# Row sums of the fifth turn: from VectorE's reduction to adds on GpSimd and one sum on TensorE, with VectorE squaring every fourth unit, in a two-layer graph kernel

## The chip, the cores and the metric

The kernel runs on one core of one Trainium2 chip. The metric is the device time of one execution in microseconds; for the kernel before it is 596.5 us, the median of three runs (594.94 to 597.69).

## The reference

Two layers over x (4096 x 128) with one dense matrix adj (4096 x 4096, float32). h is the row-normalized x, cut at zero; r is an element of adj.

```python
# layer 0
msg = h @ W + B
sens = exp(-(1.0 / r - 1.0) ** 2 / (2.0 * 0.5 * 0.5))
x = x + where(r < 1.0, sens, 0.0) @ msg
# layer 1, with h from the new x
A_hat = adj + eye(N)
d_inv_sqrt = sum(A_hat, axis=1) ** (-0.5)
x = x + relu((d_inv_sqrt[:, None] * A_hat * d_inv_sqrt[None, :]) @ (h @ W.T))
```

Layer 1 needs the row sums of adj, and it needs adj a second time, with rows of layer 1's h that exist only once layer 0 is done for those rows.

## The kernel before, in words

adj is cut into 64 units of 512 x 512 elements, held as 128 partitions x 2048. Eight turns of eight units each go through the matrix by blocks of 512 rows; turn g (counted from 0) takes the units u = 8g to 8g+7, in the column order of ORDER. The "fifth turn" is g = 4, units 32 to 39. `idx` is a unit's place in its turn. Two units are loaded as one pair into one of three buffers `raw` (SyncE's queue, 16 transfers a pair, `load`). The order of work on every engine is written out by hand in a loop over u; the engines meet only by semaphores.

For each unit:

- VectorE turns it (`turn`, line 665) from `raw` into one of four buffers `kept`, as soon as the buffer's earlier unit has been stored or used, and cuts it (`cut`, line 680): wt = v where v < 1, else 0, read as two inputs from `kept`.
- ScalarE makes the weight in place in `wt` (five buffers): logarithm (`log`, line 546), exp of its negative, which is 1/r (`invert`, line 551), the square of 1/r - 1 (`square`, line 556) and the last exp (`weigh`, line 565). For some units VectorE makes the square instead (`quad`, line 686, an operation of the shape of the cut, after `invert`), and `weigh` has another bias (line 562). `squared_by_dve` picks them: one in four of the first turn, one in two of the next three, none later.
- TensorE multiplies the weights with msg into the bank acc0, two units behind (`multiply_weights`, line 394), and in the same loop does layer 1's products (`mix_once`, line 407) for those units of `kept` whose columns are ready, or (`mix_late`, line 417) for units that were spilled to HBM and are loaded again.
- SyncE stores the units to be used again (`store`, line 307); GpSimd issues the late loads (line 362) in the order of LOADED, each after the buffer's earlier use is done (`late_done`).

The row sums are made in two ways. In the first four turns (PE_SUMS = 4) TensorE adds each unit of `kept` by a product with a matrix of ones (`sum_tiles`, line 425); ScalarE copies the bank (`copy_sums`, line 573), and TensorE turns the sums into rows (`turn_sums`, line 432). From the fifth turn on VectorE reduces each pair from `raw` (`row_sum`, line 673), and a small product (`sum_quads`, line 440) joins the parts. A `raw` buffer is free for the next load when both units are turned and, from the fifth turn on, also summed.

Between the turns stands a chain on the rows just finished: ScalarE copies acc0 (`copy_x1t`, line 591), TensorE transposes (`turn_x1`, line 448), VectorE adds to x and takes the moments (`make_x1`, lines 762 to 780), TensorE transposes again (`turn_hid`, line 454), ScalarE copies (`copy_hid`, line 603), TensorE multiplies with the second weight matrix (`multiply_support`, line 460) and VectorE scales (`make_support`, lines 690 to 791). `own_rows` (lines 748 to 756) takes the row sums up before `make_x1`. STEPS gives the place in the turn of each of these. After the last unit the remaining late units are multiplied and the eight row blocks are finished.

Of the kernel before, what the change touches and what calls it, by code (L numbers as in the profile page):

```python
# [5 lines left out]
P = 128  # L6
# [68 lines left out]


PE_SUMS = 4


def squared_by_dve(u):  # L80

    return u < PE_SUMS * G and u % (4 if u < G else 2) == (3 if u < G else 1)

# [34 lines left out]
def slot_before(j):  # L118

    return max((i for i in range(j) if late_slot(i) == late_slot(j)), default=None)  # L120


# [5 lines left out]
def build(nc, x, adj, w0, b0, w1, out):  # L128
# [6 lines left out]
    with ctx:  # L135
# [25 lines left out]
        late = sb("late", [P, LATE, T, ROWS])  # L161
        wt = sb("wt", [P, WTS, T, ROWS])
        x1t = sb("x1t", [D, ROWS])
        hid = sb("hid", [P, T, D])
# [32 lines left out]
        msg_bank = [mix[4], mix[5]]  # L197
        sum_bank = [mix[0], mix[3], mix[4], mix[5]]

# [30 lines left out]
        square_done = sem("square_done")  # L230
        quad_done = sem("quad_done")
        tiles_summed = sem("tiles_summed")
        sums_copied = sem("sums_copied")
# [53 lines left out]
        def _(sp):  # L287
            def load(n):
                g = n // C4
                if n >= RAW:  # L290
                    if n - RAW >= PE_SUMS * C4:
                        sp.wait_ge(summed, n - RAW + 1 - PE_SUMS * C4)
                    sp.wait_ge(turned, 2 * (n - RAW + 1))
                for e in range(0, 16, 4):
                    for q in (0, 2, 1, 3):
                        sp.dma_start(raw[q * B:(q + 1) * B, n % RAW, e:e + 4],  # L296
                                     adj_parts[g // 2, g % 2, col(2 * n) // 2, q, :, e:e + 4]
                                     ).then_inc(raw_loaded[n % RAW], 16)
# [36 lines left out]
        def _(pool):  # L335
# [14 lines left out]

            for j, (r, c) in enumerate(LOADED):
                slot = late_slot(j)
                u = r * G + ORDER[r].index(c)
                before = slot_before(j)
                if before is not None:
                    pool.wait_ge(late_done, before + 1)
                elif slot >= LATE:
                    last_pair = max(n for n in range(PAIRS) if n % RAW == (slot - LATE) // 2)
                    pool.wait_ge(summed, last_pair + 1 - PE_SUMS * C4)
                    pool.wait_ge(turned, 2 * last_pair + 2)  # L360
                pool.wait_ge(spilled[u % KEPT], 16 * spill_count(u))
                pool.dma_start(late_tile(slot).rearrange("p k i -> p (k i)"),  # L362
                               spill[r, c]).then_inc(late_loaded[slot], 16)

        @block.tensor
        def _(pe):
# [54 lines left out]
            def sum_tiles(u):  # L421
# [5 lines left out]
                mm.then_inc(tiles_summed, 1)  # L427

            def turn_sums(g):
                pe.wait_ge(sums_copied, g + 1)  # L430
# [5 lines left out]
            def sum_quads(g):  # L436
                pe.wait_ge(summed, C4 * (g + 1 - PE_SUMS))
                if g == PE_SUMS:
                    pe.wait_ge(quads_done, 2)
# [31 lines left out]
            for u in range(UNITS):  # L471
                g, idx = u // G, u % G
                if g == 0 and idx % 2 == 0:
                    turn_h0(idx // 2)
                    multiply_msg(idx // 2)
                if g > PE_SUMS and step_at(g, idx, "sum_quads"):
                    sum_quads(g - 1)
# [6 lines left out]
                if g >= 1 and idx < LAG:  # L484
                    multiply_weights(u - LAG)
                if 1 <= g <= PE_SUMS and step_at(g, idx, "sum_quads"):
                    turn_sums(g - 1)
# [54 lines left out]
        def _(act):  # L542
# [24 lines left out]
            def copy_sums(g):  # L567
                act.wait_ge(tiles_summed, G * (g + 1))
                if g == 0:
# [45 lines left out]
            for u in range(UNITS):  # L615
# [9 lines left out]
                if g == 0 and idx in (1, 3, 5):  # L625
                    std_rows((idx + 1) // 2)
                    copy_h0((idx + 1) // 2)
                if 1 <= g <= PE_SUMS and idx == 0:
                    copy_sums(g - 1)
# [22 lines left out]
        def _(dve):  # L652
            def turn(u):
# [3 lines left out]
                if u >= KEPT:  # L657
# [3 lines left out]
                    if at_once(v):  # L661
                        dve.wait_ge(once_done, once_count(v))
                dst = kept[:, u % KEPT].rearrange("p k (e i) -> p e k i", i=B)
                src = raw[:, n % RAW].rearrange("p e (k h i) -> p e k h i", k=T, h=2)[:, :, :, h, :]
                nc.vector.transpose(dst, src).then_inc(turned, 1)  # L665

            def row_sum(n):
                g, jp = n // C4, n % C4
                if g >= PE_SUMS + 2 and jp == 0:
                    dve.wait_ge(quads_summed, g - 1)  # L670
# [72 lines left out]
            def own_rows(g):  # L743
                dve.wait_ge(quads_summed, g + 1)
                if g >= 1:
                    dve.wait_ge(newton, 3 * g)
                if g < PE_SUMS:
                    nc.vector.tensor_copy(pows[:, 0, :], side[:, 0:T]).then_inc(rows_owned, 1)
                    dve.wait_ge(rows_owned, g + 1)
                    return  # L750
                if g == PE_SUMS:
                    dve.wait_ge(quads_done, 2)
# [6 lines left out]
            def make_x1(g):  # L759
# [16 lines left out]
                last.then_inc(hid_done, 1)  # L776
                if g >= PE_SUMS:
                    dve.wait_ge(rows_summed, g + 1 - PE_SUMS)
                nc.vector.tensor_scalar(pows[:, 0, :], pows[:, 0, :], 1.0, None, ALU.add)
# [17 lines left out]
            for u in range(UNITS):  # L797
                g, idx = u // G, u % G
                turn(u)
                if g < PE_SUMS or u < PE_SUMS * G + 2:  # L800
                    cut(u)
                    if u >= 1 and squared_by_dve(u - 1):
                        quad(u - 1)
                if idx % 2 == 1 and g >= PE_SUMS:
                    row_sum(u // 2)
# [4 lines left out]
                elif g == 0:  # L810
                    make_msg(idx // 2)
                if u >= PE_SUMS * G + 2:
                    cut(u)
# [62 lines left out]
```

## Time and profile before

| | |
|---|---|
| median of three runs | 596.5 us (594.94 to 597.69) |
| the profiled execution: its time, its span | 593.92 us, 592.1 us |
| TensorE matmul busy | 528.7 us (89%) |
| VectorE busy | 472.2 us (80%) |
| ScalarE busy | 462.4 us (78%) |
| GpSimd busy | 41.4 us (7%) |
| row sums on VectorE (line 673), 16 | 70.1 us |
| cuts on VectorE (line 680), 64 | 146.5 us |
| squares on ScalarE (line 556), 50; on VectorE (line 686), 14 | 94.9 us; 32.0 us |
| sums on TensorE (line 425), 256 records | 35.1 us |

Of the profiled execution the profile shows the busy time of each engine, the chain of work that ended last, the groups of instructions by line, and timelines. Times are from the span's start. DVE is VectorE, ACT ScalarE, PE TensorE, POOL GpSimd. A float32 matmul appears as two records, so "x8" is one unit's four products. Busy time is an average over stages with different limits.

### The profile page before, as it was taken

How to read it: one execution, taken by the hardware profiler on the slowest of the kernel's cores; microseconds unless marked ns; L12 is line 12 of the kernel's file. 1: busy time of each engine (PE TensorE's matmuls, PEld its weight loads, DVE VectorE, ACT ScalarE, POOL GpSimd, SP SyncE). 2: the span in 40 equal slices, each digit the busy share in tenths (PEclk: the TensorE clock that was granted, in tenths of full speed). 3: DMA queues.
4: the chain of work that ended last, by engine and by line, in shares of the span. 5: the costliest groups of instructions: out<-in, count | busy, mean ns of one | idle time of the engine just before them, and what ended most of it. 6: DMA issues, size and time to landing. Idle time of an engine off the chain costs nothing.

```text
span 592.1 us, 4974 instructions
## 1 busy us (share of the span) xinstructions
PE 528.7 (89%) x1579; PEld 239.3 (40%) x1579; DVE 472.2 (80%) x552; ACT 462.4 (78%) x305; POOL 41.4 (7%) x68
## 2 busy tenths in 40 slices
PE   2458796979989999999979998989999999999994
PEld 1244433323433444344434444434444444445452
DVE  5899988999899898999999599995999379003156
ACT  2299899999999999998999949999699948900010
POOL 0343300000000000000000000000000000201000
PEclk9759897999999999999979999999999999999998
DMA  6999999999999999979989959994888220399122
GB/s 170 223 234 318 331 330 336 344 326 295 367 323 339 346 344 260 303 232 355 231 192 315 254 163 251 343 261 104 213 213 214 71 71 6 137 424 361 66 71 71
DMA packets 93340, 145.19 MB, mean 245 GB/s; under 512 B 10369, under 2 KB 84354, under 8 KB 84354
## 3 DMA queue, kind: packets, MB, share of 16 engines
q1 hardware_dynamic: 88274, 108.17, 66.8%
q0 software_dynamic: 5040, 36.70, 16.6%
q8 instruction: 12, 0.20, 0.1%
q14 instruction: 14, 0.11, 0.1%
HBM read 106.04 MB, written 38.80 MB: 245 GB/s over the span
## 4 chain that ended last, share of the span: by engine, by line
PE 45%; ACT 23%; DVE 15%; SPq 8%; issue 5%; DMA 3%; DVEq 0%
PE acc L394 17%; PE mix L417 12%; PE mix L407 10%; SPq L296 7%; ACT wt L546 6%; ACT wt L551 6%; DVE kept L665 6%; ACT wt L556 5%; ACT wt L565 5%; DVE wt L680 3%; DVE rowpart L673 2%; DMA adj_t_spill<-kept 2%; PE acc L417 2%; PE mix L425 1%; DVE wt L686 1%
## 5 line engine op out<-in xcount | busy, mean ns | idle before, releaser
L394 PE MATMUL acc<-wt,msg 128*128 128x512 f32 x512 | 238.1, 609 | 15.8 <-ACT wt L565 8.9
L394 PEld LDWEIGHTS acc<-wt,msg 128*128 128x128 f32 x512 | 95.7, 193 | 146.1 <-issue 121.3
L665 DVE STREAM_TRANSPOSE kept<-raw 128x2048 f32<-128x2048 f32 x64 | 147.4, 2304 | 6.9 <-DMA adj_t_spill<-kept 5.1
L680 DVE SCALAR_TENSOR_TENSOR wt<-kept 128x2048 f32<-128x2048 f32 x64 | 146.5, 2288 | 1.7
L546 ACT ACTIVATE wt<-wt 128x2048 f32<-128x2048 f32 x64 | 121.7, 1902 | 19.9 <-DVE wt L680 19.9
L551 ACT ACTIVATE wt<-wt 128x2048 f32<-128x2048 f32 x64 | 121.6, 1900 | 0.5
L407 PE MATMUL mix<-kept,support 128*128 128x512 f32 x224 | 101.2, 595 | 1.7 <-DVE kept L665 1.7
L565 ACT ACTIVATE wt<-wt 128x2048 f32<-128x2048 f32 x50 | 95.0, 1899 | 0.0
L556 ACT ACTIVATE wt<-wt 128x2048 f32<-128x2048 f32 x50 | 94.9, 1897 | 0.0
L417 PE MATMUL mix<-late,support 128*128 128x512 f32 x208 | 93.5, 593 | 1.3 <-DVE support L791 1.3
L673 DVE TENSOR_REDUCE rowpart<-raw 128x16 f32<-128x4096 f32 x16 | 70.1, 4380 | 0.0
L407 PEld LDWEIGHTS mix<-kept,support 128*128 128x128 f32 x224 | 41.8, 190 | 54.4 <-issue 51.6
L417 PEld LDWEIGHTS mix<-late,support 128*128 128x128 f32 x208 | 39.2, 190 | 49.9 <-issue 49.9
L362 POOL DMA_DIRECT2D late<-adj_t_spill x26 | 13.9, 535 | 454.6 <-PE mix L417 375.4
L425 PE MATMUL mix<-kept,ones 128*32 128x512 f32 x256 | 35.1, 621 | 9.4 <-DVE kept L665 9.4
L762 DVE TENSOR_TENSOR x<-side,x 128x512 f32<-128x512 f32 x8 | 5.5, 686 | 43.2 <-PE side L448 43.2
L686 DVE SCALAR_TENSOR_TENSOR wt<-wt 128x2048 f32<-128x2048 f32 x14 | 32.0, 2287 | 7.0 <-ACT wt L551 6.9
L603 ACT COPY hid_t<-side 128x512 f32<-128x512 f32 x8 | 4.6, 574 | 29.5 <-PE side L454 29.5
L649 ACT COPY kept<-mix 128x512 f32<-128x512 f32 x6 | 3.5, 585 | 29.9 <-PE mix L417 26.6
L562 ACT ACTIVATE wt<-wt 128x2048 f32<-128x2048 f32 x14 | 26.5, 1895 | 0.0
L347 POOL TENSOR_SCALAR support<-x,mv 128x128 f32<-128x128 f32 x24 | 21.9, 928 | 40.1 <-DVE mv L705 40.1
L830 DVE TENSOR_TENSOR kept<-mix,support 128x512 f32<-128x512 f32 x6 | 4.1, 689 | 19.2 <-PE mix L508 19.2
(87 smaller groups left out, 254.2 us busy)
## 6 DMA issues: line engine op xcount, KB each, us to landing
raw<-in_adj_dram SPq DMA_DIRECT2D x512, 128.0 KB, 6.3
adj_t_spill<-kept SPq DMA_DIRECT2D x35, 1024.0 KB, 9.8
late<-adj_t_spill POOLq DMA_DIRECT2D x26, 1024.0 KB, 8.4
raw<-adj_t_spill POOLq DMA_DIRECT2D x9, 1024.0 KB, 9.1
x<-in_x_dram SPq DMA_DIRECT2D x32, 64.0 KB, 2.7
out_dram<-kept SPq DMA_DIRECT2D x32, 64.0 KB, 1.8
w_sb<-in_L_gnn_W_dram SPq DMA_DIRECT2D x1, 64.0 KB
late<-in_L_gnn_W_dram SPq DMA_DIRECT2D x1, 64.0 KB
```

The source lines that it names most:

```text
L296: sp.dma_start(raw[q * B:(q + 1) * B, n % RAW, e:e + 4], adj_parts[g // 2, g % 2, col(2 * n) // 2, q, :, e:e + 4]).then_inc(raw_loaded[n % ...
L394: mm = nc.tensor.matmul(acc0[:], msg[:, col(u) * T + k, :], wt[:, u % WTS, k, :], start=(first and k == 0), stop=(last and k == T - 1))
L407: mm = nc.tensor.matmul(once_bank[g][:], support[:, c * T + k, :], kept[:, u % KEPT, k, :], start=(first and k == 0), stop=False)
L417: mm = nc.tensor.matmul(bank[:], support[:, c * T + k, :], late_tile(slot)[:, k, :], start=(start and k == 0), stop=(stop and k == T - 1))
L425: mm = nc.tensor.matmul(bank[k * B:(k + 1) * B, :], ones[:], kept[:, u % KEPT, k, :], start=(u % G == 0), stop=(u % G == G - 1))
L546: nc.scalar.activation(v, v, ACT.Ln, bias=LN_GUARD).then_inc(ln_done, 1)
L551: nc.scalar.activation(v, v, ACT.Exp, scale=-1.0).then_inc(inv_done, 1)
L556: nc.scalar.activation(v, v, ACT.Square, bias=-1.0).then_inc(square_done, 1)
L565: nc.scalar.activation(v, v, ACT.Exp, scale=-2.0).then_inc(wt_done, 1)
L665: nc.vector.transpose(dst, src).then_inc(turned, 1)
L673: nc.vector.tensor_reduce(dst, src, AX_X, ALU.add).then_inc(summed, 1)
L680: nc.vector.scalar_tensor_tensor(out=wt[:, u % WTS], in0=v, scalar=CUTOFF, in1=v, op0=ALU.is_lt, op1=ALU.mult).then_inc(cut_done, 1)
```

## The change

PE_SUMS stays 4 and a second bound DVE_SUMS = 5 takes its place wherever it says from which turn on VectorE reduces the rows. In the fifth turn GpSimd adds the turned units of `kept` up in a new buffer `row_acc` (128 x 2048, float32): seven adds, the first of units 32 and 33. Each waits for its unit to be turned and for the add before. TensorE then sums `row_acc` by one product with ones into the bank mix[5] (`sum_total`) at unit 40, after the weights' product; ScalarE copies it and TensorE turns it, as in the earlier turns. VectorE's `turn` of unit u, when unit u - 4 is one that GpSimd adds, waits for that add. VectorE makes the square of the units 35 and 39. The late loads of GpSimd's queue are issued from the same loop over the units, each placed by `load_unit` at the unit after that whose product frees its buffer, before that unit's add. SyncE's loads that follow the fifth turn's pairs no longer wait for a row sum. The dynamic DMA scratch is set to 8192 bytes, half of what it was, which makes room for `row_acc`.

```diff
 PE_SUMS = 4
+DVE_SUMS = PE_SUMS + 1
+
+def added_by_pool(u):
+    return PE_SUMS <= u // G < DVE_SUMS
+
+def adds(u):
+    return max(1, u % G)
 
 def squared_by_dve(u):
-    return u < PE_SUMS * G and u % (4 if u < G else 2) == (3 if u < G else 1)
+    return u < DVE_SUMS * G and u % (4 if u < G or added_by_pool(u) else 2) == (3 if u < G or added_by_pool(u) else 1)
...
+def load_unit(j):
+    before = slot_before(j)
+    if before is None:
+        return G + 2 + j
+    return [u for u in sorted(JOBS) for _ in JOBS[u]][before] + 1
...
+        row_acc = sb("row_acc", [P, T, ROWS])
...
-        sum_bank = [mix[0], mix[3], mix[4], mix[5]]
+        sum_bank = [mix[0], mix[3], mix[4], mix[5], mix[5]]
...
-                    if n - RAW >= PE_SUMS * C4:
-                        sp.wait_ge(summed, n - RAW + 1 - PE_SUMS * C4)
+                    if n - RAW >= DVE_SUMS * C4:
+                        sp.wait_ge(summed, n - RAW + 1 - DVE_SUMS * C4)
                     sp.wait_ge(turned, 2 * (n - RAW + 1))
...
-            for j, (r, c) in enumerate(LOADED):
+            def add(u):
+                pool.wait_ge(turned, u + 1)
+                if adds(u) >= 2:
+                    pool.wait_ge(pool_added, adds(u) - 1)
+                first = kept[:, (u - 1) % KEPT] if u % G == 1 else row_acc[:]
+                nc.gpsimd.tensor_tensor(row_acc[:].rearrange("p k i -> p (k i)"),
+                                        first.rearrange("p k i -> p (k i)"),
+                                        kept[:, u % KEPT].rearrange("p k i -> p (k i)"),
+                                        ALU.add).then_inc(pool_added, 1)
+
+            def load_late(j):
+                r, c = LOADED[j]
...
+            for u in range(G, UNITS):
+                for j in range(len(IN_TURN)):
+                    if load_unit(j) == u:
+                        load_late(j)
+                if added_by_pool(u) and u % G >= 1:
+                    add(u)
+            for j in range(len(IN_TURN), len(LOADED)):
+                load_late(j)
...
+            def sum_total():
+                pe.wait_ge(pool_added, G - 1)
+                for k in range(T):
+                    mm = nc.tensor.matmul(sum_bank[PE_SUMS][k * B:(k + 1) * B, :], ones[:], row_acc[:, k, :],
+                                          start=True, stop=True)
+                mm.then_inc(tiles_summed, 1)
...
+                if u == DVE_SUMS * G:
+                    sum_total()
-                if 1 <= g <= PE_SUMS and step_at(g, idx, "sum_quads"):
+                if 1 <= g <= DVE_SUMS and step_at(g, idx, "sum_quads"):
                     turn_sums(g - 1)
...
-                act.wait_ge(tiles_summed, G * (g + 1))
+                act.wait_ge(tiles_summed, G * (g + 1) if g < PE_SUMS else G * PE_SUMS + 1)
...
-                if 1 <= g <= PE_SUMS and idx == 0:
+                if 1 <= g <= DVE_SUMS and idx == 0:
                     copy_sums(g - 1)
...
                     if at_once(v):
                         dve.wait_ge(once_done, once_count(v))
+                    if added_by_pool(v):
+                        dve.wait_ge(pool_added, adds(v))
...
-                if g < PE_SUMS or u < PE_SUMS * G + 2:
+                if g < DVE_SUMS or u < DVE_SUMS * G + 2:
                     cut(u)
                     if u >= 1 and squared_by_dve(u - 1):
                         quad(u - 1)
-                if idx % 2 == 1 and g >= PE_SUMS:
+                if idx % 2 == 1 and g >= DVE_SUMS:
                     row_sum(u // 2)
...
-    nc = _bacc.Bacc("TRN2", target_bir_lowering=False, num_devices=1)
+    nc = _bacc.Bacc("TRN2", target_bir_lowering=False, num_devices=1, dynamic_dma_scratch_size=8192)
```

In `sum_quads`, `row_sum`, `own_rows`, `make_x1` and the late loads' waits PE_SUMS becomes DVE_SUMS in the same way.

## Rows read from the trace of the kernel before

**Rows 1.** The chain of waits, 296 to 360 us: start us, us, what.

```profile
300.37 2.29 DVE wt L680
302.69 1.91 ACT wt L546
304.60 1.80 ACT wt L556
...
329.80 0.47 ACT x1t L591
330.27 0.14 issue
330.41 3.67 PE acc L394 x8
```

**Rows 2.** Stretches: busy time of each engine, granted TensorE clock, DMA.

```profile
core 0: us, PE busy (x) PEld busy (x) DVE busy (x) ACT busy (x) POOL busy (x), PEclk, DMA share, GB/s
249.00:302.00 53.00, 48.09 (x129) 22.07 (x127) 52.59 (x43) 50.04 (x32) 1.58 (x3) 0.99 0.93 260
398.00:490.00 92.00, 91.22 (x229) 41.73 (x230) 72.72 (x66) 76.40 (x49) 2.64 (x5) 1.00 0.57 147
...
302.00:308.50 6.50, 6.42 (x8) 2.75 (x9) 6.46 (x4) 5.84 (x5) 0.00 (x0) 0.52 0.98 237
```

**Rows 3.** VectorE: its groups in 253 to 303 us, then its timeline.

```profile
L673 DVE TENSOR_REDUCE rowpart<-raw 128x16 f32<-128x4096 f32 x4 | 17.6, 4388 | 0.0
L665 DVE STREAM_TRANSPOSE kept<-raw 128x2048 f32<-128x2048 f32 x7 | 16.1, 2304 | 0.0
...
251.16 2.29 DVE L680 SCALAR_TENSOR_TENSOR wt<-kept 128x2048 f32<-128x2048 f32 x1
...
271.16 0.68 DVE L762 TENSOR_TENSOR x<-side,x 128x512 f32<-128x512 f32 x1
...
274.13 2.30 DVE L665 STREAM_TRANSPOSE kept<-raw 128x2048 f32<-128x2048 f32 x1
...
287.40 0.16 DVE L690 TENSOR_TENSOR tmp<-inv 128x8 f32<-128x8 f32 x1
...
289.30 2.30 DVE L665 STREAM_TRANSPOSE kept<-raw 128x2048 f32<-128x2048 f32 x1
```

**Rows 4.** ScalarE: a group of 249 to 303 us, and its timeline.

```profile
L546 ACT ACTIVATE wt<-wt 128x2048 f32<-128x2048 f32 x8 | 15.2, 1904 | 3.6 <-DVE wt L680 3.6
...
253.83 0.57 ACT L573 COPY hid_t<-mix 128x512 f32<-128x512 f32 x1
```

**Rows 5.** TensorE's timeline, 228 to 308 us.

```profile
228.44 1.06 PE L425 MATMUL mix<-kept,ones 128*32 128x512 f32 x8
...
259.39 0.95 PE L432 MATMUL side<-thirty_second,hid_t 128*128 128x1 f32 x8
...
276.49 3.70 PE L407 MATMUL mix<-kept,support 128*128 128x512 f32 x8 [1.43 <-DVE kept L665]
...
302.08 6.76 PE L394 MATMUL acc<-wt,msg 128*128 128x512 f32 x8 [3.29 <-ACT wt L565]
```

**Rows 6.** GpSimd's timeline, the first 2 us.

```profile
0.24 0.10 POOL L865 MEMSET const-float32-0.0<- 128x1 f32 x1 [0.24 <-issue]
...
0.74 0.20 POOL L336 MEMSET ident<- 128x128 f32 x1 [0.29 <-POOLq L865]
...
1.22 0.28 POOL L341 TENSOR_SCALAR_AFFINE_SELECT ident<-ident 128x128 f32<-128x128 f32 x1
```

**Rows 7.** GpSimd's line 347 (ns min/median/max); 28 to 29 us of it; VectorE beside it.

```profile
L347 POOL TENSOR_SCALAR support<-x,mv x24: 702/710/2474, 24.7 to 62.8; 128x128 f32<-128x128 f32 x24
...
L347 POOL TENSOR_SCALAR support<-x,mv 128x128 f32<-128x128 f32 x1 | 2.5, 2452 | 0.0
...
27.06 2.29 DVE L680 SCALAR_TENSOR_TENSOR wt<-kept 128x2048 f32<-128x2048 f32 x1
```

**Rows 8.** GpSimd's timeline, late loads of the fifth turn.

```profile
256.42 0.53 POOL L362 DMA_DIRECT2D late<-adj_t_spill  x1 [41.10 <-PE mix L417]
264.18 0.53 POOL L362 DMA_DIRECT2D late<-adj_t_spill  x1 [7.23 <-PE mix L417]
271.49 0.53 POOL L362 DMA_DIRECT2D late<-adj_t_spill  x1 [6.78 <-PE mix L417]
```

More of the change, by code:

```diff
@@ L231, in build @@
         quad_done = sem("quad_done")
+        pool_added = sem("pool_added")
         tiles_summed = sem("tiles_summed")
@@ L358, in _ @@
                     last_pair = max(n for n in range(PAIRS) if n % RAW == (slot - LATE) // 2)
-                    pool.wait_ge(summed, last_pair + 1 - PE_SUMS * C4)
+                    pool.wait_ge(summed, last_pair + 1 - DVE_SUMS * C4)
                     pool.wait_ge(turned, 2 * last_pair + 2)
@@ L436, in sum_quads @@
             def sum_quads(g):
-                pe.wait_ge(summed, C4 * (g + 1 - PE_SUMS))
-                if g == PE_SUMS:
+                pe.wait_ge(summed, C4 * (g + 1 - DVE_SUMS))
+                if g == DVE_SUMS:
                     pe.wait_ge(quads_done, 2)
@@ L475, in _ @@
                     multiply_msg(idx // 2)
-                if g > PE_SUMS and step_at(g, idx, "sum_quads"):
+                if g > DVE_SUMS and step_at(g, idx, "sum_quads"):
                     sum_quads(g - 1)
@@ L668, in row_sum @@
                 g, jp = n // C4, n % C4
-                if g >= PE_SUMS + 2 and jp == 0:
+                if g >= DVE_SUMS + 2 and jp == 0:
                     dve.wait_ge(quads_summed, g - 1)
@@ L746, in own_rows @@
                     dve.wait_ge(newton, 3 * g)
-                if g < PE_SUMS:
+                if g < DVE_SUMS:
                     nc.vector.tensor_copy(pows[:, 0, :], side[:, 0:T]).then_inc(rows_owned, 1)
@@ L750, in own_rows @@
                     return
-                if g == PE_SUMS:
+                if g == DVE_SUMS:
                     dve.wait_ge(quads_done, 2)
@@ L776, in make_x1 @@
                 last.then_inc(hid_done, 1)
-                if g >= PE_SUMS:
-                    dve.wait_ge(rows_summed, g + 1 - PE_SUMS)
+                if g >= DVE_SUMS:
+                    dve.wait_ge(rows_summed, g + 1 - DVE_SUMS)
                 nc.vector.tensor_scalar(pows[:, 0, :], pows[:, 0, :], 1.0, None, ALU.add)
@@ L811, in _ @@
                     make_msg(idx // 2)
-                if u >= PE_SUMS * G + 2:
+                if u >= DVE_SUMS * G + 2:
                     cut(u)
```

## The prediction

> **What bounds the kernel now.** I read the chain of waits first, then the stretches, then the timelines of single engines around the fifth turn (units 32 to 39). Up to the cut of unit 39 the chain lies on VectorE; it then passes to ScalarE, whose work is back to back until the copy of x1's transpose, and at 330.4 us to TensorE [rows 1]. From there TensorE is the limit for most of what is left (in 398 to 490 us it is busy 91.2 of 92 us [rows 2]), so a shift of the point 330.4 moves the end by about as much. In 249 to 302 us VectorE is busy 52.6 of 53 us, TensorE 48.1, ScalarE 50.0 [rows 2]. There VectorE makes four row sums of 4.4 us, 17.6 in all, and its transposes wait for nothing, so neither loads nor spills are late [rows 3]. ScalarE loses 3.6 us to late cuts in that turn [rows 4]. TensorE stands idle 3.3 us before unit 37's product, which then takes 6.76 us where unit 36's at 276.49 took 3.70 [rows 5]: the granted clock is 0.52 there, the lower of its two levels [rows 2]. That is 3.1 us more, though TensorE catches up: at 330.4 it waits 0.75 us for ScalarE (the chain's copy ends at 330.3).
>
> **The change, part by part.** *VectorE*: minus four row sums, 17.6 us; plus two squares of the cut's shape, 2 x 2.3 = 4.6. Net 13.0 us less, if nothing holds it. *ScalarE*: minus two squares of 1.8 us (the steps of the chain [rows 1]); plus one copy of the sums, 0.5 [rows 4]; and the 3.6 us of waits go if cuts are on time: at most 3.6 + 3.6 - 0.5 = 6.7 us before the copy of x1's transpose in unit 42's place. *TensorE*: plus one sum of the total, 1.06, and the turning of the sums, 0.95; minus a small product of the partial sums, taken as nothing: +2.0 us [rows 5]. Against that stand the 3.3 us idle, the 3.1 of low clock and the 1.4 us it waited for unit 36's transpose [rows 5], 7.8 in all: TensorE could be 5.8 us early, plus the 0.75 it waits: 6.5. *Halved scratch*: descriptor space of GpSimd's DMAs; no row shows it full or waited for. I take nothing; a loss would fall on the burst of loads at the end.
>
> *GpSimd*: seven adds of 128x2048. The trace has none. Its memset of one element takes 0.10 us and of 128 elements 0.20, so 0.8 ns for an element written; the select of 128, one read and one write, 0.28, so 1.4 ns [rows 6], and 0.6 for the read. Two reads and a write: 2.0 ns x 2048 = 4.2 us. Ends: 2.3 us, if it ran as fast as VectorE's cut [rows 7], and 11.2, sixteen times the 0.70 us that its tensor_scalar of 128 elements takes [rows 7], nearly all of it a fixed part. I take 4.2, from the rows nearest in kind. At 7.2 us a unit (four chain steps of ScalarE) GpSimd keeps up.
> The Trainium skill (GPSIMD Engine Reference, section 3) gives 4.5 us for exactly this add; by it the sum below would be 1.5 us longer. No row here shows it.
>
> *Order on GpSimd's queue*: the adds of units 33, 34 and 35 stand behind the late loads 6, 7 and 8, which wait for TensorE and go out at 256.4, 264.2 and 271.5 [rows 8]. So these adds begin from 257.0, 264.7 and 272.0. VectorE's new waits (unit 36 may not overwrite its buffer before unit 32 is added, and so on) lie 7 us and more behind these, and cost nothing while an add is under 7 us. TensorE's sum of the total waits for the last add and stands behind unit 38's product, about 314 us; the last add ends by 307. The next late load (job 9) has its turn after that.
>
> *Sharing between GpSimd and VectorE*, the term that decides. Eight tensor_scalars of GpSimd run beside VectorE; in each batch one takes 2.47 us instead of 0.70, and it is the one in flight during the cut, which takes its usual 2.29 [rows 7]. So a cut (two inputs in SBUF) shuts GpSimd out until it ends. Whether GpSimd, once reading, shuts the cut out, no row shows: the instruction in flight as the cut began can have finished its 128 reads. Lower bound: no delay to VectorE. Upper bound: a whole add for each add that meets a cut or a square. Since the port is visibly held for a whole instruction and not shared element by element, I take it to be held both ways.
> The Trainium skill (SBUF — State Buffer, "Who interferes with whom") says that whoever issues first has the shared pair for its whole instruction and that two SBUF inputs contend with GpSimd's reads. Rows 7 agree for the one direction. It speaks against this change.
>
> **The sum with the port held both ways, add 4.2 us.** Start at the cut of unit 33, 251.2 [rows 3]; without row sums, transpose and cut are 4.55 us a unit. Unit 34's cut ends at 258.0; add 33 holds the port to 262.2. Unit 35's cut waits for the previous turn's sums (TensorE from 259.4, a little under 0.95 us [rows 5]) and ends at 265.0; add 34 to 269.2, beside make_x1, 3.0 us (271.16 to 274.13 [rows 3]), and transpose 36. Cut 36 ends 272.5, add 35 holds to 276.7, then square 35 (whose input ScalarE has ready by about 275) to 279.0, add 36 to 283.2, cut 37 to 285.5, add 37 to 289.7. The small two-input steps of make_support meet that and its 1.9 us (287.40 to 289.30 [rows 3]) begin only then: 291.6. Cut 38 ends 296.1, add 38 at 300.3, cut 39 at 302.6: 302.66 now [rows 1]. So the four row sums taken away are given back whole. On: add 39 to 306.8, cut 40 to 309.0, square 39 to 311.3, cut 41 to 315.8, the row sum of the sixth turn's first pair to 320.1, cut 42 to 324.6. ScalarE takes up unit 42 at 324.65; now it does 5.4 us (three steps) before 329.8, at 324.4. Shift +0.3. TensorE would idle again before units 38's and 37's products and pay low clock once more, but reaches 330.4 just in time. Sum: 593.9 (the profiled execution) + 0.4 = 594.3; that execution is 2.6 below the median of the three runs, so against the median 596.5 + 0.4, about **596.9**. Five adds in a row lie on this path (35 to 39), so it moves by 5 us for each microsecond of the add: 4.5 gives +1.8, 3.7 gives -2.2.
>
> **Rivals.** *VectorE is never held by GpSimd* (adds fit in the gaps). Then cut 39 is done by about 293, well before ScalarE wants it, and square 39 waits for ScalarE's inverse at 302.7: cut 41 ends at 309.5, and after row sum and transpose cut 42 at 318.4, while ScalarE, 6.7 us early, would take it at 324.4 - 6.7 = 317.7. The loss of 0.7 leaves 6.0 us, and TensorE's 6.5 lets that stand: 596.5 - 6.0 = **590.5**. For: all three cuts that began beside a GpSimd instruction took 2.29. Against: the shut-out in the other direction is complete.
> *A long add, both ways held* (the slower side). Mechanism: the chain add, cut, add of units 35 to 39. It decides from where (A - 4.2) x 5 passes 3 us, an add of 4.8. At 5.5 us: +6.5 + 0.4, **603.4**; an idle TensorE at low clock could add its 3.1. For: GpSimd's spans here have big fixed parts (0.70 for 128 elements). Against: GpSimd's memset and select scale gently.
> *GpSimd too late altogether*: an add of over 7.2 us would stall VectorE's transposes at unit 38 on; each microsecond above costs at least five. Toward the upper end of 11.2 that is over 620. I give this 2 in 100.
>
> **How the numbers follow.** About 0.5% (3 us) is what a measurement of this kernel can tell from no change. Held both ways with an add of 3.7 to 4.8: 0.50, own range 594 to 600, of it 0.06 faster, 0.36 same, 0.08 slower. Never held: 0.36, own range 588.5 to 593.5, of it 0.33 faster, 0.03 same. Long add: 0.12, slower; too late 0.02, slower. Together faster 0.39, same 0.39, slower 0.22. Same and faster weigh alike; I forecast the single likeliest case, 596.9. The range must reach the never-held case, and leaves out its lowest part and the long adds above 5.2 us: 589 to 602.
>
> **What would show it.** In the changed profile: cuts and squares of the fifth turn longer than 2.29 us or beginning over 2 us after the transpose; GpSimd adds of 4.2 us and, where they meet a cut, 6.5; spacing of transposes near 7 us in spite of the missing row sums; the cut of unit 39 ending near 302 against 293 in the never-held case. The step at 330.4 shifts by under 3 us or by -6. ScalarE's waits for cuts stay near 3.6 us or vanish. I am wrong in the mechanism if cuts keep 2.29 with no gap while adds run, and wrong in a term if adds alone take over 5 or under 3.5. If the time falls or rises with the first 330 us unchanged, it lies in the tail, and the scratch or the order of the late loads would be suspect.

## The result, and the profile after

The changed kernel takes 602.04 us (median of four, 598.1 to 604.31) where the kernel before, run beside it, takes 596.3. The ratio is 1.0098, 95% interval 1.0068 to 1.0128: slower by 5.8 us. The forecast was 596.9, range 589 to 602; the time lies above it.

The profiled execution of the changed kernel is the fastest of its four (598.1 us); its span is 596.3 us, that of the kernel before 592.1. Its fifth turn begins earlier: unit 32's transpose starts at 239.64, in the trace before at 240.96. Single executions differ by more than that up to there (unit 34's transpose starts at 252.06 here, and at 254.32 in a kernel below that has the same program so far). So 1.3 us are added to the times after when the two are compared.

VectorE's groups of the changed kernel in 249 to 303 us (columns as in [rows 3]):

```profile
L733 DVE SCALAR_TENSOR_TENSOR wt<-kept 128x2048 f32<-128x2048 f32 x7 | 21.9, 3123 | 0.2
L718 DVE STREAM_TRANSPOSE kept<-raw 128x2048 f32<-128x2048 f32 x7 | 16.1, 2302 | 0.0
L739 DVE SCALAR_TENSOR_TENSOR wt<-wt 128x2048 f32<-128x2048 f32 x1 | 6.6, 6624 | 0.0
L743 DVE TENSOR_TENSOR tmp<-inv 128x8 f32<-128x8 f32 x1 | 4.5, 4516 | 0.0
L827 DVE TENSOR_SCALAR hid<-x,mv 128x128 f32<-128x128 f32 x4 | 3.1, 838 | 0.0
```

The row sums are gone. In their place a cut (line 733) takes 3.12 us on average, the square of unit 35 (line 739) 6.62 and a step on 8 elements (line 743) 4.52. VectorE's timeline, with unit 36 first:

```profile
265.85 3.12 DVE L827 TENSOR_SCALAR hid<-x,mv 128x128 f32<-128x128 f32 x4
...
269.04 2.29 DVE L718 STREAM_TRANSPOSE kept<-raw 128x2048 f32<-128x2048 f32 x1
271.37 6.09 DVE L733 SCALAR_TENSOR_TENSOR wt<-kept 128x2048 f32<-128x2048 f32 x1
277.38 6.62 DVE L739 SCALAR_TENSOR_TENSOR wt<-wt 128x2048 f32<-128x2048 f32 x1
283.93 2.30 DVE L718 STREAM_TRANSPOSE kept<-raw 128x2048 f32<-128x2048 f32 x1
286.26 2.29 DVE L733 SCALAR_TENSOR_TENSOR wt<-kept 128x2048 f32<-128x2048 f32 x1
288.47 4.52 DVE L743 TENSOR_TENSOR tmp<-inv 128x8 f32<-128x8 f32 x1
...
297.07 2.29 DVE L733 SCALAR_TENSOR_TENSOR wt<-kept 128x2048 f32<-128x2048 f32 x1
...
301.62 4.31 DVE L733 SCALAR_TENSOR_TENSOR wt<-kept 128x2048 f32<-128x2048 f32 x1
```

And GpSimd's timeline beside it: add 34, the late load ahead of add 35, then adds 35, 36 and 37 one by one:

```profile
263.45 4.85 POOL L378 TENSOR_TENSOR row_acc<-row_acc,kept 128x2048 f32<-128x2048 f32 x1
270.17 0.57 POOL L395 DMA_DIRECT2D late<-adj_t_spill  x1 [1.87 <-PE mix L459]
270.76 4.54 POOL L378 TENSOR_TENSOR row_acc<-row_acc,kept 128x2048 f32<-128x2048 f32 x1
275.44 6.41 POOL L378 TENSOR_TENSOR row_acc<-row_acc,kept 128x2048 f32<-128x2048 f32 x1
286.31 6.65 POOL L378 TENSOR_TENSOR row_acc<-row_acc,kept 128x2048 f32<-128x2048 f32 x1 [4.46 <-DVE kept L718]
```

Lay the two side by side. Add 35 starts at 270.76, 0.6 us ahead of cut 36; the cut ends when the add's 4.5 us and its own 2.2 have gone by. Add 36's record starts at 275.44; it waits for the cut to end at 277.5 and then runs to 281.85; only then does square 35 run, which ends at 284.0, 6.6 us after it started. Where VectorE comes first it is GpSimd that waits: add 37 starts with cut 37 and takes 6.65 us. Line 378's shortest add, never held, is the 4.54 us of unit 35. Not every operation is held: beside add 34 the addition to x (0.68 us) and the statistics (0.87 for four) take what they took before, and transposes keep 2.30 us beside the adds.

The sum up to the end of cut 38, against the trace before: three row sums less (3 x 4.3 = 12.9), one square more (2.3), a new wait of 2.4 us for the previous turn's sums at unit 34, and held time of 3.8 (cut 36), 4.3 (square 35), 2.3 (hid) and 4.4 us (line 743), 14.8 in all: 14.8 + 2.4 + 2.3 - 12.9 = 6.6. Measured: 299.36 + 1.3 against 293.93 is +6.7. TensorE follows:

```profile
286.28 5.40 PE L449 MATMUL mix<-kept,support 128*128 128x512 f32 x8 [4.78 <-DVE kept L718]
291.52 3.60 PE L436 MATMUL acc<-wt,msg 128*128 128x512 f32 x8
297.09 3.70 PE L449 MATMUL mix<-kept,support 128*128 128x512 f32 x8 [1.98 <-DVE kept L718]
...
306.76 5.40 PE L436 MATMUL acc<-wt,msg 128*128 128x512 f32 x8 [2.53 <-ACT wt L616]
...
318.95 1.06 PE L474 MATMUL mix<-row_acc,ones 128*32 128x512 f32 x8
...
334.68 3.60 PE L436 MATMUL acc<-wt,msg 128*128 128x512 f32 x8
```

The last product starts unit 40's weights; it answers to 330.41 in [rows 1] and comes 4.3 + 1.3 = 5.6 us later. Most of that is ScalarE's lateness, which comes from the cuts: its copy of x1's transpose starts at 333.55, in the trace before at 329.71, which is 5.1 us later. The last 0.5 us is TensorE's: from 306.76 on it has no gap, with the sum of the total and the turning of the sums added (1.8 us), while the product at 306.76 is 1.8 us slow (5.40 against 3.60) where it was 3.1 before. The granted clock of the 6 us with that product is 0.72 on average, so a part of them lies at the lower of the two levels (columns as in [rows 2]):

```profile
306.00:312.00 6.00, 5.24 (x9) 2.23 (x10) 5.96 (x2) 6.00 (x4) 4.33 (x1) 0.72 1.07 247
```

From there to the end nothing is added: the span is 4.2 us longer, plus 1.3 is 5.5, close to the 5.8 of the ratio.

### The profile page after: what moved, and what is told of

The parts are those of the page before. It is cut to its first block, busy times and chain, and to the rows that moved or that the text cites. A ratio compares the mean times of both kernels' runs of the same rounds, so it can differ in the third digit from the quotient of the medians.

```text
span 596.3 us, 5012 instructions
## 1 busy us (share of the span) xinstructions
PE 532.4 (89%) x1593; PEld 239.1 (40%) x1593; DVE 478.4 (80%) x549; ACT 459.9 (77%) x304; POOL 82.5 (14%) x75
## 4 chain that ended last, share of the span: by engine, by line
PE 54%; ACT 18%; DVE 13%; SPq 6%; DMA 4%; issue 2%; POOL 2%; DVEq 0%; POOLq 0%
PE acc L436 21%; PE mix L459 14%; PE mix L449 12%; SPq L318 5%; ACT wt L597 5%; ACT wt L602 5%; DVE kept L718 4%; ACT wt L616 4%; ACT wt L607 4%; DVE wt L733 3%; DMA adj_t_spill<-kept 3%; DVE wt L739 2%; PE mix L467 2%; POOL row_acc L378 2%; PE acc L459 2%
## 5 line engine op out<-in xcount | busy, mean ns | idle before, releaser
L733 DVE SCALAR_TENSOR_TENSOR wt<-kept 128x2048 f32<-128x2048 f32 x64 | 154.3, 2412 | 1.8
L449 PE MATMUL mix<-kept,support 128*128 128x512 f32 x224 | 102.9, 603 | 6.8 <-DVE kept L718 6.8
L726 DVE TENSOR_REDUCE rowpart<-raw 128x16 f32<-128x4096 f32 x12 | 52.6, 4381 | 0.0
L739 DVE SCALAR_TENSOR_TENSOR wt<-wt 128x2048 f32<-128x2048 f32 x16 | 40.9, 2558 | 7.1 <-ACT wt L602 7.0
L467 PE MATMUL mix<-kept,ones 128*32 128x512 f32 x256 | 36.7, 647 | 7.4 <-DVE kept L718 7.4
L378 POOL TENSOR_TENSOR row_acc<-row_acc,kept 128x2048 f32<-128x2048 f32 x6 | 35.5, 5920 | 8.9 <-DVE kept L718 8.6
```

Of the source, the lines that this page charges most:

```text
L449: mm = nc.tensor.matmul(once_bank[g][:], support[:, c * T + k, :], kept[:, u % KEPT, k, :], start=(first and k == 0), stop=False)
L467: mm = nc.tensor.matmul(bank[k * B:(k + 1) * B, :], ones[:], kept[:, u % KEPT, k, :], start=(u % G == 0), stop=(u % G == G - 1))
L726: nc.vector.tensor_reduce(dst, src, AX_X, ALU.add).then_inc(summed, 1)
L733: nc.vector.scalar_tensor_tensor(out=wt[:, u % WTS], in0=v, scalar=CUTOFF, in1=v, op0=ALU.is_lt, op1=ALU.mult).then_inc(cut_done, 1)
L739: nc.vector.scalar_tensor_tensor(out=v, in0=v, scalar=-2.0, in1=v, op0=ALU.add, op1=ALU.mult).then_inc(quad_done, 1)
```

## Experiments

The theory: GpSimd and VectorE share a way into SBUF (the port, below) that one instruction holds; a GpSimd instruction that reads holds up those of VectorE's that need it. The rivals put the loss on what else changed: the order on GpSimd's queue, the new waits, the halved scratch, TensorE's added work, the squares. Each ratio below is to the kernel before on the same chip, with its 95% interval.

**Adds of 128 elements.** (On the changed kernel, as all that follow unless the text says otherwise.) The other 1920 elements of each unit's sums are left out.

```diff
-                nc.gpsimd.tensor_tensor(row_acc[:].rearrange("p k i -> p (k i)"),
-                                        first.rearrange("p k i -> p (k i)"),
-                                        kept[:, u % KEPT].rearrange("p k i -> p (k i)"),
-                                        ALU.add).then_inc(pool_added, 1)
+                nc.gpsimd.tensor_tensor(row_acc[:, 0, 0:128], first[:, 0, 0:128],
+                                        kept[:, u % KEPT, 0, 0:128], ALU.add).then_inc(pool_added, 1)
```

> The changed kernel, but each of GpSimd's seven adds covers only 128 of the 2048 elements (the rest of the fifth turn's row sums is left out; the total is filled with ones at the start). Everything else of the change stays: the order of the late loads on GpSimd's queue, the new waits, TensorE's sum of the total, the halved scratch, VectorE's two squares. Theory (an add of GpSimd that has begun holds VectorE's two-input operations until it ends): nothing long is held, cuts and squares of the fifth turn are back at 2.29 us, and the time falls below the kernel before, to about 590.5 us (ratio to before 0.99). Rival (the loss comes from what stays): about 602 us, ratio 1.01.

Measured: 589.83 us, ratio 0.9909 (0.9876 to 0.9941). Line 734 is the cut, min/median/max in ns over all 64; then the groups of the square, of hid and of the small step in 245 to 302 us:

```profile
L734 DVE SCALAR_TENSOR_TENSOR wt<-kept x64: 2276/2292/2294, 20.1 to 495.5; 128x2048 f32<-128x2048 f32 x64
```

```profile
L740 DVE SCALAR_TENSOR_TENSOR wt<-wt 128x2048 f32<-128x2048 f32 x2 | 4.6, 2293 | 3.0 <-ACT wt L603 3.0
...
L828 DVE TENSOR_SCALAR hid<-x,mv 128x128 f32<-128x128 f32 x4 | 0.9, 283 | 0.0
...
L744 DVE TENSOR_TENSOR tmp<-inv 128x8 f32<-128x8 f32 x1 | 0.4, 422 | 0.0
```

No cut is held. Everything else of the change together is a gain of 0.9%, and the length of the adds costs about 11 us (1.0098 against 0.9909). This is the prediction's never-held case, 590.5. It throws out the rivals of scratch, TensorE's work and the order of issue. Small adds also end VectorE's new waits sooner and let the late loads through sooner; that these are not the cause is read from the trace with the full adds: VectorE has no idle time before any transpose of the fifth turn, and GpSimd, its adds done, still waits for TensorE before each late load (1.87 us before the one at 270.17, 13.6 before the first one after the adds).

**The scratch alone**, on the kernel before.

```diff
-    nc = _bacc.Bacc("TRN2", target_bir_lowering=False, num_devices=1)
+    nc = _bacc.Bacc("TRN2", target_bir_lowering=False, num_devices=1, dynamic_dma_scratch_size=8192)
```

> The kernel before with nothing changed but the dynamic DMA scratch halved to 8192 bytes. Theory: no change, ratio 1.000 within 0.3%, and the nine or so late loads issued at the end keep their 0.53 us spacing. Rival (smaller descriptor space delays GpSimd's loads): slower by 2 us or more, with longer load instructions in the last 90 us.

Measured: 595.12 us, ratio 0.9988 (0.9972 to 1.0003). The nine loads into `raw` at the end take 530 ns each, before 528. No cost can be told.

**Adds of 1024 elements.** Half of the fifth turn's sums is left out.

```diff
-                nc.gpsimd.tensor_tensor(row_acc[:].rearrange("p k i -> p (k i)"),
-                                        first.rearrange("p k i -> p (k i)"),
-                                        kept[:, u % KEPT].rearrange("p k i -> p (k i)"),
-                                        ALU.add).then_inc(pool_added, 1)
+                nc.gpsimd.tensor_tensor(row_acc[:, 0:2].rearrange("p k i -> p (k i)"),
+                                        first[:, 0:2].rearrange("p k i -> p (k i)"),
+                                        kept[:, u % KEPT, 0:2].rearrange("p k i -> p (k i)"),
+                                        ALU.add).then_inc(pool_added, 1)
```

> As the changed kernel, but each add covers 1024 of 2048 elements (half of the fifth turn's row sums is left out). An add then takes about 2.3 us, and fits beside a transpose of 2.3 us. Theory (port held both ways): most cuts are not held or by under 1 us, time 591 to 594 us. A loss that grows in proportion to GpSimd's busy time would give halfway between 590.5 and 602, 596 us. Rival (the loss comes from what stays): 602 us.

Measured: 590.94 us, ratio 0.9931 (0.9908 to 0.9953). VectorE, the square of unit 35 and the small step:

```profile
280.06 2.46 DVE L742 SCALAR_TENSOR_TENSOR wt<-wt 128x2048 f32<-128x2048 f32 x1 [1.92 <-ACT wt L605]
...
286.99 2.33 DVE L746 TENSOR_TENSOR tmp<-inv 128x8 f32<-128x8 f32 x1
```

The holds are still there but short, 0.2 and 2.2 us, and VectorE has idle time to take them in (1.9 us before the square). The loss is not proportional to GpSimd's work: half the work costs some 1 us, which is within the two intervals, all of it about 11.

**A fill instead of an add, and a copy instead of an add.** Both leave the fifth turn's row sums out; the copy has one run.

The line that stands in the add's place, in the one kernel and in the other:

```diff
+                nc.gpsimd.memset(row_acc[:], 1.0).then_inc(pool_added, 1)
```

```diff
+                nc.gpsimd.tensor_copy(row_acc[:].rearrange("p k i -> p (k i)"),
+                                      kept[:, u % KEPT].rearrange("p k i -> p (k i)")).then_inc(pool_added, 1)
```

> As the changed kernel, but in place of each add GpSimd fills the 128x2048 buffer with a constant (the fifth turn's row sums are left out): a long GpSimd instruction that writes SBUF and reads nothing. If what is held is the reading side of the port, cuts and squares keep 2.29 us and the time is that of the tiny adds, about 590.5 us. If any long GpSimd instruction holds VectorE (writing side too), cuts stretch by what is left of the fill (estimated at 1.6 us from the 0.8 ns an element of the small fills) and the time lies at 592 to 595 us; if the loss is of the waits and the order, 602 us.

> As the changed kernel with a plain copy of each unit by GpSimd in place of the add (the fifth turn's row sums are left out): one input instead of two. If one read stream is enough to hold VectorE, the first small step of make_support, which takes 0.16 us in the kernel before, 0.16 with the fills and 4.52 with the full adds, takes 1 to 3 us, about as long as the copy; if only two inputs hold it, 0.16. Time 590 to 593 us in both cases.

Measured: the fill 590.39 us, ratio 0.9901 (0.9872 to 0.993); the copy 589.27. The seven fills (min/median/max in ns), unit 36's fill, and VectorE's square of unit 35, which starts while that fill runs:

```profile
L377 POOL MEMSET row_acc<- x7: 1806/1809/1828, 260.2 to 294.2; 128x2048 f32 x7
...
277.24 1.81 POOL L377 MEMSET row_acc<- 128x2048 f32 x1
```

```profile
278.01 2.29 DVE L735 SCALAR_TENSOR_TENSOR wt<-wt 128x2048 f32<-128x2048 f32 x1 [2.00 <-ACT wt L598]
```

The seven copies, and VectorE's timeline with the square of unit 35 and the small step:

```profile
L377 POOL COPY row_acc<-kept x7: 1896/2811/4017, 256.7 to 293.4; 128x2048 f32<-128x2048 f32 x7
```

```profile
274.50 3.93 DVE L736 SCALAR_TENSOR_TENSOR wt<-wt 128x2048 f32<-128x2048 f32 x1 [1.99 <-ACT wt L599]
...
282.90 1.85 DVE L740 TENSOR_TENSOR tmp<-inv 128x8 f32<-128x8 f32 x1
```

A fill of 1.81 us, which only writes, holds no cut or square and is held by none: the square above keeps 2.29 us, and the longest fill is 0.02 us longer than the shortest although some start beside cuts. (The small step, 0.16 us here, says nothing: the fill before it, 282.58 to 284.39, was over when it started at 284.77.) A copy, one read stream, both holds (the small step 1.85 us, the square 3.93) and is held (up to 4.02 us, against 1.90). So what is shared is on the reading side, and one stream on GpSimd's side is enough. The times do not tell the two apart, as expected; the durations do.

**The squares back on ScalarE**, the rest as changed.

```diff
-    return u < DVE_SUMS * G and u % (4 if u < G or added_by_pool(u) else 2) == (3 if u < G or added_by_pool(u) else 1)
+    return u < PE_SUMS * G and u % (4 if u < G else 2) == (3 if u < G else 1)
```

> The changed kernel without one part: ScalarE squares units 35 and 39 again, VectorE does not. Theory (an add holds two-input operations): in the changed kernel the square of unit 35 alone is held to 6.62 us and the cut behind it waits as well; without it the cut of unit 38 ends about 4.5 us earlier although ScalarE has 3.6 us more to do, most of it while it waited anyway: about 598 us, ratio to before 1.00. Rival (squares on VectorE are the useful part of the change, the adds the loss): 604 to 606 us.

Measured: 597.8 us, ratio 1.0039 (1.0022 to 1.0057). Cut 36 and cut 37:

```profile
273.64 6.11 DVE L733 SCALAR_TENSOR_TENSOR wt<-kept 128x2048 f32<-128x2048 f32 x1
279.68 2.30 DVE L718 STREAM_TRANSPOSE kept<-raw 128x2048 f32<-128x2048 f32 x1
282.01 4.32 DVE L733 SCALAR_TENSOR_TENSOR wt<-kept 128x2048 f32<-128x2048 f32 x1
```

Taking the squares away gives back some 3.5 of the 5.8 us (1.0098 to 1.0039), a little less than the theory's 4.5; cut 37 is now held by add 36 instead, for 2.0 us, since the transpose covers the rest. Here moving the squares to VectorE is a loss while full adds run beside them.

**Adds in two and in four pieces.** All sums computed. The edit for two pieces stands here; for four, 2 becomes 1.

```diff
+                for i in range(0, T, 2):
+                    last = nc.gpsimd.tensor_tensor(row_acc[:, i:i + 2].rearrange("p k i -> p (k i)"),
+                                                   first[:, i:i + 2].rearrange("p k i -> p (k i)"),
+                                                   kept[:, u % KEPT, i:i + 2].rearrange("p k i -> p (k i)"),
+                                                   ALU.add)
+                last.then_inc(pool_added, 1)
```

> The changed kernel, all of its sums computed, but each add is issued as two instructions of 1024 elements, about 2.3 us each. Theory (the port is held for one instruction and passed on when it ends): a cut waits for at most 2.3 us, VectorE has some 2 us to spare per unit where ScalarE sets the pace, so little of it shows: 592 to 596 us, ratio to before 0.993 to 1.0. Rival (GpSimd keeps the port as long as it has adds queued, or the loss follows GpSimd's total busy time, which stays): 602 us.

> As the last, with four instructions of 512 elements, about 1.2 us each and 0.1 to 0.3 us more for issuing them. Theory: a VectorE operation waits for at most 1.2 us; 591 to 594 us, ratio 0.99 to 0.995, at or below the two-part adds. If each instruction's fixed part (0.7 us for 128 elements) counts in full, GpSimd's adds take about 7 us a unit, VectorE's transposes come to wait for them: 600 us or more. Rival as before: 602 us.

Measured: 599.68 us, ratio 1.0067 (1.0044 to 1.009), and 600.1 us, ratio 1.0077 (1.0056 to 1.0098). Here the theory's detail failed: a cut was to wait for one piece at most. GpSimd's two pieces of unit 35's add, one by one, and VectorE's cut 36 and square 35, in two pieces:

```profile
274.30 2.38 POOL L379 TENSOR_TENSOR row_acc<-row_acc,kept 128x1024 f32<-128x1024 f32 x1
...
276.62 2.38 POOL L379 TENSOR_TENSOR row_acc<-row_acc,kept 128x1024 f32<-128x1024 f32 x1
```

```profile
274.85 6.31 DVE L735 SCALAR_TENSOR_TENSOR wt<-kept 128x2048 f32<-128x2048 f32 x1
281.09 4.45 DVE L741 SCALAR_TENSOR_TENSOR wt<-wt 128x2048 f32<-128x2048 f32 x1
```

The cut waits through both pieces, 4.0 us, although the first ends at 276.7. With four pieces the same cut takes 6.48 us. But the square behind it waits for one piece only (4.45 us in two pieces, 3.36 in four). So in these two traces pieces that follow one another without having been held keep VectorE out like one long add, while after GpSimd has itself been held the two take turns. Why it is so these runs do not show. In four pieces a plain copy of VectorE, 4 elements from SBUF to SBUF, is held too (0.17 us alone):

```profile
291.34 1.20 DVE L841 COPY dinv<-inv 128x4 f32<-128x4 f32 x1
```

Splitting gained 1 to 2 us of the 5.8, not the 6 to 11 that were expected, and the intervals overlap with that of the whole adds.

**Adds ahead of the late loads** on GpSimd's queue.

```diff
             for u in range(G, UNITS):
+                if added_by_pool(u) and u % G >= 1:
+                    add(u)
                 for j in range(len(IN_TURN)):
                     if load_unit(j) == u:
                         load_late(j)
-                if added_by_pool(u) and u % G >= 1:
-                    add(u)
```

> The changed kernel with each add ahead of the late load of the same unit on GpSimd's queue, so that the adds of units 33 to 35 are released by their transposes and not by TensorE. Theory (what is held depends on who comes first): add 35 then begins after cut 35 and no longer stands in front of cut 36 and the moments' steps; the cut of 36 (6.09 us in the changed kernel) shortens to 2.3 to 4.5 us, the cut of unit 38 ends 2 to 4 us earlier: 598 to 600 us. Rival (the port's total load decides, whatever the order): 602 us. Late loads 6 to 8 go out up to 5 us later; if TensorE comes to wait for them, above 602 us.

Measured: 599.66 us, ratio 1.0069 (1.0042 to 1.0096). VectorE:

```profile
257.14 4.32 DVE L733 SCALAR_TENSOR_TENSOR wt<-kept 128x2048 f32<-128x2048 f32 x1
...
264.34 3.69 DVE L733 SCALAR_TENSOR_TENSOR wt<-kept 128x2048 f32<-128x2048 f32 x1
...
275.52 2.29 DVE L733 SCALAR_TENSOR_TENSOR wt<-kept 128x2048 f32<-128x2048 f32 x1
277.73 6.63 DVE L739 SCALAR_TENSOR_TENSOR wt<-wt 128x2048 f32<-128x2048 f32 x1
```

Cut 36 falls from 6.09 to 2.29 us, and the cuts of units 34 and 35 are held instead, 2.0 and 1.4 us; the first falls into time that VectorE stood idle before (2.4 us, now 0.3). hid and square 35 are held as before (3.13 and 6.63 us). The order on the queue decides what is held. In the trace the cut of unit 38 ends 2.4 us sooner after unit 34's transpose; the two ratios' intervals overlap, so the time alone does not show it.

**The fifth turn's sums on TensorE alone** (a change of the kernel before: GpSimd out of it, VectorE squaring 35 and 39; units 32 and 33 are summed at unit 33, behind `turn_sums`, since ScalarE still reads the bank before; a transpose waits for the sum of the buffer's earlier unit).

```diff
-PE_SUMS = 4
+PE_SUMS = 5
...
+                if u == 33:
+                    sum_tiles(32)
+                    sum_tiles(33)
```

> The kernel before with the fifth turn's row sums on TensorE alone, as in the first four turns (units 32 and 33 summed at unit 33), VectorE squaring units 35 and 39 as in the change, GpSimd out of it. VectorE and ScalarE gain what the never-held case gave them (6.0 us), TensorE pays 8 sums of 1.0 us instead of its idle 3.3 and low clock 3.1 and waits of 1.4. Theory (without GpSimd's port nothing is held; TensorE becomes the bound of that turn): cuts 2.29 us, about 596 us or 1 less, ratio 0.995 to 1.0. If TensorE had more room than its idle time shows: 590.5 us. If TensorE's extra work costs in full on top of its old waits: 601 us.

Measured: 594.92 us, ratio 0.9987 (0.9963 to 1.001). The stretch of 249 to 302 us (columns as in [rows 2]):

```profile
249.00:302.00 53.00, 53.00 (x180) 22.51 (x179) 42.03 (x43) 48.87 (x32) 1.59 (x3) 1.00 1.01 279
```

TensorE is busy all of it, with a granted clock of 1.00 (its level of 2.4 GHz), and VectorE falls to 42.0 of 53 us, its cuts all at 2.29. The bound has gone to TensorE, and the gain is spent there: no change from the kernel before can be told.

**Shared by elements**: GpSimd adds 1024 elements of each unit, TensorE sums the other 1024. All sums computed.

```diff
+            def sum_half(u):
+                for k in (2, 3):
+                    mm = nc.tensor.matmul(sum_bank[PE_SUMS][k * B:(k + 1) * B, :], ones[:], kept[:, u % KEPT, k, :],
+                                          start=(u % G == 0), stop=(u % G == G - 1))
```

> All sums computed: GpSimd adds only the first 1024 elements of each unit of the fifth turn (2.3 us an add), TensorE sums the other 1024 (half a unit's sum, 0.5 us, eight times) and the total. Theory: holds are as rare as with the half adds alone (590.9 us), and TensorE pays 3.5 us more, of which about 0.7 shows, as in the all-TensorE version (7 us more work, 4.9 us longer than the tiny adds): 592.5 to 593.5 us, ratio to before 0.995. Rival (TensorE's and GpSimd's costs add up in full): 595 us, no better than all on TensorE.

Measured: 597.04 us, ratio 1.0026 (1.0008 to 1.0044), above the theory's 593 and the rival's 595. What stands out is on TensorE, two of the halves:

```profile
278.69 1.05 PE L475 MATMUL mix<-kept,ones 128*32 128x512 f32 x4
...
283.74 1.05 PE L475 MATMUL mix<-kept,ones 128*32 128x512 f32 x4
```

Two products into two groups of 32 rows take 1.05 us, as long as four into four groups (1.06 in [rows 5]). Half the sum saves TensorE nothing: it is busy 53.0 of the 53 us again, as in the version before, and the sum of the total and the short adds' holds (2.4 us on the square of 35) come on top. That these make up the 2 us over the version before was not tested.

**Shared by units**: TensorE sums units 32 to 35, GpSimd adds 36 to 39. All sums computed.

```diff
 def adds(u):
-    return max(1, u % G)
+    return max(1, u % G - G // 2)
...
-                if added_by_pool(u) and u % G >= 1:
+                if added_by_pool(u) and u % G >= G // 2 + 1:
                     add(u)
```

A product like `sum_tiles` sums units 32 to 35 into the bank, which stays open for the total.

> All sums computed: TensorE sums units 32 to 35 of the fifth turn (four sums of 1.0 us), GpSimd adds up units 36 to 39 (three adds of 4.5 us) and TensorE sums their total into the same bank. Theory: the holds at the moments' steps, the cut of unit 36 and the square of unit 35 are gone; what is left is one add on the first small step of make_support (4.5 us) and the two on the cuts of 39 and 40. TensorE has 4 us more to do than in the changed kernel and no idle before unit 36's product. The cut of unit 38 ends some 6 us earlier than in the changed kernel: 594 to 597 us, ratio to before 0.995 to 1.002. Rival (each add costs the same wherever it lies: 12 us over seven adds): 590.5 + 3 x 1.7 + 3 = 598.5 us.

Measured: 593.88 us, ratio 0.9956 (0.9932 to 0.9979). Cut 36, square 35 and the small step:

```profile
274.50 2.29 DVE L752 SCALAR_TENSOR_TENSOR wt<-kept 128x2048 f32<-128x2048 f32 x1
276.71 2.29 DVE L758 SCALAR_TENSOR_TENSOR wt<-wt 128x2048 f32<-128x2048 f32 x1
...
283.46 4.51 DVE L762 TENSOR_TENSOR tmp<-inv 128x8 f32<-128x8 f32 x1
```

The holds of unit 36 are gone; those at the small step and on the cuts of 39 and 40 (4.32 us each) are left. This beats both kernels, the one before by 0.4%, the changed one by 1.4%; a gain of 2.6 us, against the 5.4 of the tiny adds (0.9909), which are held up by nothing long.

## Why the prediction was wrong

It forecast no change, 596.9 us, and the time rose by 5.8 us. The mechanism it took was right; the order in which it laid the operations at the port was not.

- *The mechanism* was right: the port is held both ways. Its signs are there: stretched cuts and squares, and adds of 6.65 us where a cut came first. The case without holds was given 590.5 us; tiny adds give 589.8 and fills 590.4 us.
- *The add* was taken as 4.2 us, from GpSimd's small fills and select; it takes 4.54. The prediction's own slope, five adds on the path, makes that 1.7 us; in the trace less of it shows, since add 36 still ended on schedule and from cut 37 to cut 42, with three more adds between, the lateness grew by 0.4 us only. The Trainium skill (GPSIMD Engine Reference, section 3) has 4.5 us, and the trace agrees with it (4.54). The bounds of 2.3 and 11.2 us were of no use; GpSimd's fill is 0.9 ns an element here (1.81 us for 2048), its copy also (1.90), against 2.2 for the add.
- *The step that failed* is the one that laid add 34 "beside make_x1" and let cut 36 go ahead of add 35. The scaled difference in make_x1 (hid, four instructions of 128 elements with one tensor input) took 3.12 us instead of 0.87: it is held by add 34 too. That moved cut 36 from 270.2, 1.8 us ahead of add 35 in the prediction, to 271.37 + 1.3 = 272.7, 0.6 us behind it. So cut 36 was held 3.8 us, and add 36 went before square 35. The adds themselves kept the schedule: add 36 ended at 281.85 + 1.3 = 283.2, as predicted. But square 35 (2.2 us), which was to be done before it, and transpose 37 (2.3), which was to run beside it, now stood behind it. The prediction had cut 37 end at 285.5; it ended at 288.6 + 1.3 = 289.9. These 4.4 us are most of the miss, and they stayed: cut 42 ended 4.8 us late. That hid is held by an add is read from the traces: 3.12, 3.06, 3.16 and 3.13 us wherever an add stands there, 0.88 with the sums shared by units, where none does, and 0.28 us for each of the four with the tiny adds; the prediction had counted only operations with two inputs.
- *The small steps* of make_support were held by add 37, as the prediction said (4.52 us).
- *TensorE* was said to reach 330.4 "just in time". It did not have the time: idle 4.8, 2.0 and 2.5 us before three products, it had no gap after 306.76, with its two new products behind. That is the smaller part: at 330.4's place the shift was 5.6 us where +0.3 stood (written as +0.4 in the sum), 5.1 of it ScalarE's and 0.5 TensorE's.
- *Taken as nothing*: the halved scratch (0.9988), and the new waits of VectorE's transposes, none of which shows as an idle time before line 718. Both hold.
- The Trainium skill (SBUF — State Buffer, "Who interferes with whom") gives the rule of the shared read interface; the trace agrees in both directions (6.09 us for a cut behind an add, 6.65 for an add behind a cut), and the fills agree with its word that an instruction that only writes does not contend with two-input ones (1.81 us, unheld). Its rule that whoever comes first holds the port "for the whole instruction" covers what the whole adds did, not what the pieces did.

## What to carry to other kernels

Work given to GpSimd that reads SBUF is not beside VectorE but in turn with it: count its whole length, 4.5 us for an add of 128x2048, against every VectorE operation that reads SBUF twice and, as these traces show, against a scaled difference (3.12 us for 0.87) and a plain copy (1.20 for 0.17) from SBUF to SBUF, and look which operation stands at the port when it starts. It was free where VectorE transposed (2.30 us beside adds), took statistics or was idle for as long; here one add of 2.3 us per unit was nearly free and one of 4.5 us cost 1.6 us each (11 us over seven). Put such adds where the row shows the gap, and give the rest to an engine beside which the cuts keep their time, as they did beside TensorE's sums (2.29 us).

## What the runs showed that was not expected

- An operation with one input is held too: hid took 3.12 us instead of 0.87 beside an add.
- A GpSimd add is held 2.1 us (6.65 against 4.54) by a cut of 2.29, and the square of unit 35 was held for 4.3 us although it stood directly behind a cut of its own engine: the waiting add went in between.
- Two GpSimd instructions queued without a wait kept VectorE out for both (cut of 6.31 us); after a hold, the engines took turns instruction by instruction (4.45 us).
- Two TensorE products with ones, each into 32 rows of its own, took 1.05 us together, four took 1.06.
- Half a sum on GpSimd cost some 1 us of 11. An add of 2.3 us fits beside a transpose of 2.3, one of 4.5 us does not; only these two lengths and the tiny one ran, so where the loss begins is not shown.
